# Node work between an attention and the edge sums of a graph network: two looped stages made into one written-out pipeline over 26 tiles

## The reference, cut to what matters

```python
# end of L0: agg = sum over a node's edges of alpha * message, (n, 256)
out = _typed_matmul(agg, a_linears, node_type)        # one of 4 weights, by the node's type
out = sigmoid(skip)[node_type][:, None] * out
x = x + out                                           # called x1 in the kernel

# L1, on h = relu(layernorm(x1)); row, col = src, dst
xt = (h @ weight).reshape(-1, 4, 64)
alpha_l = einsum('ehd,hd->eh', xt[row], attn_l)
alpha_r = einsum('ehd,hd->eh', xt[col], attn_r)
alpha = softmax(leaky_relu(alpha_l + alpha_r, 0.01), axis=1)     # over the 4 heads
tmp = einsum('nh,nhd->nd', alpha[:n], xt[col[:n]])    # only the first n = 3125 edges count
x = x + tmp broadcast over the 4 heads                # x2

# start of L2, on h = relu(layernorm(x2)), called h2
hs = h * rsqrt(clip(deg_out, 1))[:, None]             # rows that the edge sums gather (table2)
m = segment_sum(hs[src], dst) ...                     # sum_items, not changed
```

## Time and profile before

| | us |
|---|---|
| median of 3 timed runs | 6702.11 (6691.39 to 6745.78) |
| the profiled execution, its own time | 6654.7 |
| its span | 6653.1 |
| TensorE (PE) busy in the span | 4281.8 (64%) |
| VectorE (DVE) busy | 3563.9 (54%) |
| ScalarE (ACT) busy | 2224.7 (33%) |
| GpSimd (POOL) busy | 3118.9 (47%) |

### The profile page before, as it was taken

The page is one execution under the profiler, slowest core; times in us unless marked ns, Lnnn a source line. Parts: engine busy times, 40 slices in busy tenths (PEclk is TensorE's granted clock), DMA queues, the critical chain, the costliest instruction groups (busy, mean ns, idle before and its releaser), DMA issues. The chain is left out here.

```text
span 6653.1 us, 94389 instructions
## 1 busy us (share of the span) xinstructions
PE 4281.8 (64%) x25484; PEld 3173.8 (48%) x25484; DVE 3563.9 (54%) x7285; ACT 2224.7 (33%) x7694; POOL 3118.9 (47%) x3164
## 2 busy tenths in 40 slices
PE   3898577777767305655555558884657677776754
PEld 2665455656545204443443447772225555555542
DVE  3454688888863442222221311114249999998875
ACT  1332466666652210000000112221115555555540
POOL 0340677777750127777777020002036666666620
PEclk8999788888889656677776879995668888888875
DMA  5333788888871224333334067832147777777752
GB/s 184 119 131 116 224 260 260 253 255 260 254 173 57 59 76 123 103 103 104 104 104 97 9 213 261 262 113 84 63 149 221 222 228 223 229 226 220 224 130 73
DMA packets 559988, 1092.90 MB, mean 164 GB/s; under 512 B 129764, under 2 KB 372456, under 8 KB 556061
## 3 DMA queue, kind: packets, MB, share of 16 engines
q0 software_dynamic: 204144, 617.42, 32.2%
q1 hardware_dynamic: 355434, 470.78, 21.7%
HBM read 973.54 MB, written 201.47 MB: 177 GB/s over the span
## 5 line engine op out<-in xcount | busy, mean ns | idle before, releaser
L738 POOL DMA_INDIRECT l3e_kv<-t_table,k_recs x912 | 986.9, 1082 | 489.0 <-issue 250.7
L1394 PE MATMUL l2e_pA<-l2e_row,l2e_oh 128*128 128x257 f32 x1824 | 691.1, 545 | 742.7 <-issue 474.3
L738 POOL DMA_INDIRECT l0e_kv<-t_table,k_recs x912 | 966.9, 1060 | 292.3 <-issue 258.1
L1348 POOL DMA_INDIRECT l2e_row<-t_table,l2e_idx x912 | 882.3, 967 | 278.5 <-issue 277.5
L1394 PEld LDWEIGHTS l2e_pA<-l2e_row,l2e_oh 128*128 128x128 f32 x1824 | 472.2, 271 | 961.3 <-issue 870.4
L1015 ACT ACTIVATE l0e_vw<-l0e_kv,l0e_w 128x64 f32<-128x64 f32 x2736 | 679.8, 334 | 0.1
L1015 ACT ACTIVATE l3e_vw<-l3e_kv,l3e_w 128x64 f32<-128x64 f32 x2736 | 679.8, 334 | 0.0
L924 PE MATMUL l3e_pQE<-l3e_qb,l3e_ohT 128*128 128x256 bf16 x2736 | 412.1, 311 | 389.7 <-issue 359.4
L1373 DVE SCALAR_TENSOR_TENSOR l2e_acc<-l2e_acc,k_itf,l2e_pA 128x257 f32<-128x257 f32 x228 | 109.9, 482 | 929.4 <-issue 872.6
L972 PE MATMUL l0e_pA<-l0e_vw,l0e_ohf 128*128 128x260 f32 x1824 | 545.4, 451 | 11.0 <-ACT l0e_vw L1015 7.8
L924 PEld LDWEIGHTS l3e_pQE<-l3e_qb,l3e_ohT 128*128 128x128 bf16 x2736 | 290.9, 109 | 485.7 <-issue 410.7
(11 more groups left out here) (456 smaller groups left out, 7447.4 us busy)
## 6 DMA issues: line engine op xcount, KB each, us to landing
exp_w<-in_L_gnn_w SPq DMA_DIRECT2D x224, 512.0 KB
t_table<-l0n_tab SPq DMA_DIRECT2D x26, 2048.0 KB, 6.9
l0e_qb<-t_q SPq DMA_DIRECT2D x228, 192.0 KB, 6.0
l3e_qb<-t_q SPq DMA_DIRECT2D x228, 192.0 KB, 4.1
t_agg<-l0e_acc SPq DMA_DIRECT2D x228, 130.0 KB
t_agg<-l3e_acc SPq DMA_DIRECT2D x228, 130.0 KB
l0e_drow<-t_drow SPq DMA_DIRECT2D x57, 512.0 KB, 6.5
l3e_drow<-t_drow SPq DMA_DIRECT2D x57, 512.0 KB, 6.3
```

The source lines that it names most:

```text
L738: pool.indirect_dma_start(kv[:, n % SK, g, :], None, table[:, :], bass.IndirectOffsetOnAxis(ap=K["recs"][:, n, g, ridx:ridx + 1], axis=0)) ...
L1348: pool.indirect_dma_start(row[:, s, g, 0:D], None, table[:, :], bass.IndirectOffsetOnAxis(ap=idx[:, i, g:g + 1], axis=0)).then_inc(row_rea ...
L1394: last = pe.matmul(pA[s % 2][:, 0:W], oh[:, s, g, :], row[:, s, g, :], start=(g == 0), stop=(g == G - 1))
```

## The change

`layer1_nodes` and `layer2_nodes` are replaced by one stage, `layer12_nodes`, written out over the 26 tiles instead of looping over 13 pairs.

- x1 stays on chip in `M["xx"]`, the tile that `route` uses later; the normalised rows go into `M["agg"]`, and h2 is left in `M["h2"]`. The masks and `rdego` are kept in `K` from `layer0_nodes` on, so the store of `dego`, the stores and loads of x1 and h2 and the later loads of the masks go (in `sum_items`, `combine` and per tile). `tmask` is still stored, for `layer0_nodes` itself.
- `ag` and x are loaded in 5 chunks (`AT`) of up to 6 tiles. `wx`, `att` and the edge ends are issued by ScalarE; the edge ends as two transfers of 3328 single numbers.
- The typed projection: VectorE only divides by the denominator, a chunk at a time (`scale`); 2 transposes a tile instead of 8; `pO` holds the products with all 4 weights (2 banks), and VectorE adds the four, each times its mask column, to x (`typed`: 4 scalar_tensor_tensor). The relu is done by ScalarE in the copy of the transposed h.
- The engines' programs are shifted against each other: in slot t TensorE transposes tile t, projects tile t - 1, transposes h of t - 3, projects it for t - 4.
- GpSimd waits for all table stores, then issues 52 gathers with no wait between them. VectorE works on groups of 4 tiles (`GT`): `scores`, `heads_mean`, `normal2`; ScalarE applies relu twice per tile (`positive`).

```diff
-            with nc.allow_non_contiguous_dma(reason="3328 degrees, once"):
-                sp.dma_start(T["rdego"].rearrange("(b p) c -> p (b c)", p=P), dego[:, :]).then_inc(stored, 16)
...
-            sp.wait_ge(stored, 32)
+            sp.wait_ge(stored, 16)
...
+def layer12_nodes(nc, A, T, K, M):
...
+        AT = (0, 2, 8, 14, 20, NBP)
+        GT = (0, 4, 8, 12, 16, 20, 24, NBP)
...
+        @block.sync
+        def _(sp):
+            for j, (a, b) in enumerate(zip(AT, AT[1:])):
+                sp.dma_start(big[:, a:b, 0:H * HV], chunk("agg0", a, b)).then_inc(ag_in[j], 16)
+                if j == 0:
+                    for c in range(2):
+                        sp.dma_start(wa[:, c, :, :], A["L0_gnn_a_linears"][:, c * P:(c + 1) * P, :].rearrange("t p n -> p t n")).then_inc(wa_in, 16)
+                sp.dma_start(x[:, a:b, :], chunk("x0", a, b)).then_inc(x_in[j], 16)
+            for t in range(NBP):
+                sp.wait_ge(tb_ready, t + 1)
+                sp.dma_start(rows(T["table1"], t * P), tb[:, t % TB, :]).then_inc(tb_out[t % TB], 16)
+                sp.dma_start(rows(T["tablel"], t * P), tb[:, t % TB, D:D + H]).then_inc(tb_out[t % TB], 16)
+            for j, (a, b) in enumerate(zip(GT, GT[1:])):
+                sp.wait_ge(x2_ready, j + 1)
+                sp.dma_start(chunk("x2", a, b), x[:, a:b, :]).then_inc(stored, 16)
+                sp.wait_ge(hs_ready, j + 1)
+                sp.dma_start(chunk("table2", a, b), hs[:, j % 2, 0:b - a, :]).then_inc(hs_out[j % 2], 16)
...
+        def _(pool):
+            pool.wait_ge(edges_in, 32)
+            for u in range(TB):
+                pool.wait_ge(tb_out[u], 32 * ((NBP - 1 - u) // TB + 1))
+            for t in range(NBP):
+                j = t // GW
+                pool.indirect_dma_start(gd[:, t, :], None, T["table1"][:, :], bass.IndirectOffsetOnAxis(ap=di[:, t:t + 1], axis=0)).then_inc(g_in[j], 16)
+                pool.indirect_dma_start(gs[:, t, :], None, T["tablel"][:, :], bass.IndirectOffsetOnAxis(ap=si[:, t:t + 1], axis=0)).then_inc(g_in[j], 16)
...
+            def typed(t):
+                j = next(j for j in range(NA) if t < AT[j + 1])
+                dve.wait_ge(x_in[j], 16)
+                dve.wait_ge(o_ps, t + 1)
+                for k in range(NT):
+                    last = dve.scalar_tensor_tensor(out=x[:, t, :], in0=pO[t % 2][:, k, :], scalar=K["mask"][:, t, 1, k:k + 1], in1=x[:, t, :],
+                                                    op0=ALU.mult, op1=ALU.add)
...
+            scale(0)
+            head_weights()
+            for t in range(NBP + 2):
+                for j in range(1, NA):
+                    if t == max(AT[j] - 4, 1):
+                        scale(j)
+                if 0 <= t - 1 < NBP:
+                    typed(t - 1)
+                if 0 <= t - 2 < NBP:
+                    normal(t - 2)
...
+            for j in range(NG + 1):
+                if j < NG:
+                    scores(j)
+                if j:
+                    normal2(j - 1)
+                if j < NG:
+                    heads_mean(j)
...
+            def outputs(t):
+                pe.wait_ge(aT_ready, t + 1)
+                if t >= 2:
+                    pe.wait_ge(x1_ready, t - 1)
+                for o in range(2):
+                    for c in range(2):
+                        last = pe.matmul(pO[t % 2][:, 2 * o:2 * o + 2, :].rearrange("p k n -> p (k n)"), aT[:, t % 2, c, :],
+                                         wa[:, c, 2 * o:2 * o + 2, :].rearrange("p k n -> p (k n)"), start=(c == 0), stop=(c == 1))
+                last.then_inc(o_ps, 1)
...
+            for t in range(NBP + 4):
+                if t < NBP:
+                    turned(t)
+                if t == 1:
+                    pe.wait_ge(wa_in, 32)
+                if 0 <= t - 1 < NBP:
+                    outputs(t - 1)
+                if 0 <= t - 3 < NBP:
+                    turned_h(t - 3)
+                if t == 4:
+                    pe.wait_ge(wx_ready, 1)
+                if 0 <= t - 4 < NBP:
+                    projected(t - 4)
...
+            act.dma_start(wx[:, :, 0:D], A["L1_gnn_weight"].rearrange("(c p) n -> p c n", p=P)).then_inc(wx_in, 16)
...
+            with nc.allow_non_contiguous_dma(reason="the ends of the first 3328 edges, once"):
+                for t, a in ((si, "src"), (di, "dst")):
+                    act.dma_start(t[:, :], A[a][0:NP].rearrange("(b p) -> p b", p=P)).then_inc(edges_in, 16)
+
+            def turned(t):
...
-            sp.dma_start(M["h2"][:, :, :], T["h2"].rearrange("(b p) n -> p b n", p=P)).then_inc(next_in, 16)
-            sp.dma_start(M["mk"][:, :, :], T["tmask"].rearrange("(b p) c -> p b c", p=P)).then_inc(next_in, 16)
...
-            sp.dma_start(mk[:, :, :], T["tmask"].rearrange("(b p) c -> p b c", p=P)).then_inc(c_in, 16)
```

More of the change, by code:

```diff
@@ L1072, in layer1_nodes @@
         pH = S.ps("pH", [P, 4, P])
         pX = [S.ps(f"pX{u}", [P, 512]) for u in range(2)]
[L1074 to L1078, removed]
+        wa_in, wx_in, edges_in, wx_ready, scaled = (S.sem(k) for k in ("wa_in", "wx_in", "edges_in", "wx_ready", "scaled"))
@@ L1079, in layer1_nodes, with chunk @@
+        hs_out = S.sems_of("hs_out", 2)
         block = S.block()
+        def chunk(name, a, b):
+            return T[name].rearrange("(b p) c -> p b c", p=P)[:, a:b, :]
         @block.sync
         def _(sp):
[L1083 to L1111, removed]
@@ L1130, in step @@
[L1130 to L1149, removed]
@@ L1151, in _, with scale @@
-            repeat(dve, NBP // 2, step)
+            def scale(j):
+                a, b = AT[j], AT[j + 1]
+                dve.wait_ge(ag_in[j], 16)
+                dve.tensor_scalar(rden[:, a:b, :], ag[:, a:b, :, DK], 1e-30, None, ALU.max)
+                dve.drain()
+                dve.reciprocal(rden[:, a:b, :], rden[:, a:b, :])
+                dve.drain()
+                dve.tensor_tensor(h[:, a:b, :].rearrange("p b (h d) -> p b h d", h=H), ag[:, a:b, :, 0:DK],
+                                  rden[:, a:b, :].unsqueeze(3).to_broadcast([P, b - a, H, DK]), ALU.mult).then_inc(scaled, 1)
@@ new lines, in head_weights @@
+            def head_weights():
+                dve.wait_ge(wx_in, 48)
+                for c in range(2):
+                    for j in range(2):
+                        dve.tensor_tensor(wtmp[:, c, j, :], wx[:, c, 0:D], att[:, j, :], ALU.mult)
+                dve.drain()
+                for c in range(2):
+                    for j in range(2):
+                        last = dve.tensor_reduce(wx[:, c, D + j * H:D + (j + 1) * H], wtmp[:, c, j, :].rearrange("p (h d) -> p h d", h=H), AX.X, ALU.add)
+                last.then_inc(wx_ready, 1)
@@ new lines, in normal2 @@
+            def normal2(j):
+                a, b = GT[j], GT[j + 1]
+                dve.wait_ge(root2_ready, j + 1)
+                dve.reciprocal(mv2[:, a:b, 3], mv2[:, a:b, 2])
+                dve.drain()
+                for t in range(a, b):
+                    dve.tensor_scalar(h[:, t, :], x[:, t, :], mv2[:, t, 0:1], mv2[:, t, 3:4], ALU.subtract, ALU.mult).then_inc(n_ready, 1)
+            for j in range(NG + 1):
[5 more added lines that the diff above has]
+                    heads_mean(j)
@@ new lines, in turned_h, with projected @@
+            def turned_h(t):
+                pe.wait_ge(h_ready, t + 1)
+                if t:
+                    pe.wait_ge(hT_ready, t)
+                for c in range(2):
+                    last = pe.transpose(pH[:, c, :], h[:, t, c * P:(c + 1) * P], K["ident"][:, :])
+                last.then_inc(h_ps, 1)
+            def projected(t):
+                pe.wait_ge(hT_ready, t + 1)
+                if t >= 2:
+                    pe.wait_ge(tb_ready, t - 1)
+                for c in range(2):
+                    last = pe.matmul(pX[t % 2][:, 0:WX], hT[:, t % 2, c, :], wx[:, c, :], start=(c == 0), stop=(c == 1))
+                last.then_inc(x_ps, 1)
@@ new lines, in projected @@
+            def projected(t):
+                act.wait_ge(x_ps, t + 1)
+                if t >= TB:
+                    act.wait_ge(tb_out[t % TB], 32 * (t // TB))
+                act.activation(tb[:, t % TB, :], pX[t % 2][:, 0:WX], ACT.Copy).then_inc(tb_ready, 1)
+            for t in range(NBP + 4):
+                if t < NBP:
+                    turned(t)
+                if 0 <= t - 2 < NBP:
+                    rooted(t - 2)
+                if 0 <= t - 3 < NBP:
+                    turned_h(t - 3)
+                if 0 <= t - 4 < NBP:
+                    projected(t - 4)
```

317 lines of the change are left out of this document (135 added, 182 removed).

## The result

| | before | after |
|---|---|---|
| median of the runs first shown, us | 6699.26 (4 runs) | 6394.82 (4 runs, 6391.19 to 6416.98) |
| the profiled execution | 6654.7 | 6391.2 (span 6389.5) |

The ratio is 0.9555, 95% interval 0.9514 to 0.9595.

A forecast was written before the change was run, and what follows sets the result against it. No engine was full; chains of waits set the 506 us of node work. Gains of 252 us there and 17.5 elsewhere took 6654.7 to 6385, shifted by 47 to 6432 us; range 6365 to 6490.

The forecast's parts named there:

- stretch: From the first transfer of `layer12_nodes` to the start of `sum_items`: 254 us against 506, 252 us gained.
- Head: First transfer of the new stage to its first `pO`, ScalarE's queue held by single-number loads: 21 us.
- Steady part: The slots of the 26 tiles after the first `pO`, TensorE bounding each at 4.95 us: 135 us.
- Turn: From the last `pO` on, GpSimd waiting for every table store before gathering: 10 us with nothing beside it.
- Phase 2: 52 gathers back to back beside VectorE's groups of four tiles, VectorE just the later: 88 us.
- Degree store: End of `layer0_nodes` without the `dego` store, which took 19.5 us to land: 13.5 us gained (12 to 15).
- combine: In `combine`, where the mask load stood ahead of the x2 load: 3 us gained (0 to 6).
- The shift of 47 us: Whole kernel: timed runs' median 47 us above the profiled execution, so the sum went from 6385 to 6432 us.
- A: Head and feed slow, loads number by number crowding the chunk stream: 6455 to 6460 us; chance 0.10.
- B: TensorE loses its clock in the new slots: 6452 us at 0.90, 6561 at 1.2 GHz; chance 0.10.
- C: Pipeline doesn't overlap, in-order engines waiting for each other in every slot, 9.6 us each: 6553 us; chance 0.04.
- D: Gathers starve beside a packed VectorE, 2.83 + 0.30 us each: 6527 us; chance 0.03.

The follow-up runs named there:

- Experiment 1: Changed kernel without the shift between engines, every engine doing all steps of a tile before the next: 6674.7 us, stretch 457.1 us.
- 2: Changed kernel with half the typed projection on TensorE left out: `pO` every 3.38 to 3.52 us, typed projections 96.7 us.
- 3: Changed kernel with GpSimd waiting, before each group's eight gathers, for x2 of the group before: phase 2 131.5 us (88.9).
- 6: Changed kernel with the edge-end loads issued by GpSimd instead of ScalarE: first `pO` after 12.8 us (13.9), stretch 251.1 us.
- 12: Changed kernel with `tm` and `al` in PSUM, `normal2` ahead of `scores`, edge ends issued by GpSimd: 6393.42 us, ratio to before 0.9545.
- 4: Changed kernel with `tm` and `al` in PSUM: gathers 64.7 us in all, phase 2 84.7 us.
- 5: Changed kernel with `tm` alone in PSUM: gathers 68.1 us in all, phase 2 86.7 us.
- experiment 8: Changed kernel with the store of `dego` put back: last table store to first gather 25.4 us, against 11.0 in the changed kernel.
- Experiment 9: Changed kernel with h2 and the masks through DRAM again: phase 2 105.5 us (103.1 in the set), `sum_items` 1321.4, `combine` 115.7.

## Why the prediction was right, and which terms were off

- **The mechanism** held: stretch 237.9 to 239.0 where I had 254 (and said 245 to 265 for "right"). Experiment 1 shows the overlap, 2 that TensorE sets the slot, 3 the back-to-back gathers.
- **The sum came out near partly by luck.** On the profile's scale I had 269.5 us gained and the profiles give 263.6, but the terms miss both ways: the stretch gave 16.4 more, the end of `layer0_nodes` 9.5 less, the first attention lost 6.4 that I had at nothing, and all behind the stretch lost 2.4 where I had 4 gained.
- **One reading of before was wrong.** I put 480.6 us of GpSimd's waiting into `layer2_nodes`, which lasted 251. Its last gather of the attention ended at 1936.6, so of the 306.5 us ahead of its first gather only some 4 lie in that stage; inside it GpSimd waited some 178 us. No term of the sum used the 480.6.
- **Head** 13.9 for 21. The step "ScalarE's queue is held" is in the trace (10.65 us for my 13.6), but I added 5 us of sharing on top, which no run shows. The queue set the end; the landing of the weights stood right behind it, due one to two microseconds earlier (experiments 6 and 12). The value near the lower bound was the right choice, with the 15.6 us of before as the nearest row.
- **Steady part** 121.9 for 135. The slot is 4.77, not 4.95: near the 4.7 I gave for the case that all tails overlap. The first and the last slots, with nothing of h to transpose or project, are shorter (3.65 and 4.08 us for the second and third), which I did not count: some 4 us. One `scale` lump shows (a slot of 5.45), not four.
- **Turn** 13.1 for 10. Left without work between dependent steps, TensorE ran the last projections at a granted clock of 0.78 over the turn; the last store, issued at 2131.57, let the first gather go at 2135.20.
- **Phase 2** 88.9 for 88, but partly by luck. "VectorE just the later, over 90% busy" was wrong: 65% busy, a group 9.6 us rather than 10.7, and GpSimd sets the pace, with gathers at a mean of 1.04 for my 1.00. That 1.00 came from `combine`, where the long gathers are held in the same way (experiments 4 and 5). Here the long ones add 4.8 us, 0.09 to the mean of 52.
- **Degree store** 13.5: measured 14 (experiment 8). In the first profile only 4.0 were left, since the last table store went out 9.8 us later, at 663.27 for 653.45, in a `layer0_nodes` granted 0.76 from 150 to 200 us where the one before had 1.00.
- **sum_items** 1: lost 1.3. **combine** 3: gained 0.8. Experiment 9 prices all this traffic at 3.
- **The shift of 47 us** was the term that missed most: the changed kernel's median lies 3.6 us above its profile, not 47, which is 43 us of a miss of 37 in all. I took a gap between one profile and three runs as a property of the scale. For the larger part it was a state of `layer0_nodes` in that execution (33.8 of the 54.4 us between the two profiles of before); the rest is spread over the later stages. The first gain between medians was 304, the second 281; the profiles' own 263.6 and 289.4.
- **Rivals.** A fell (head 13.9). B did not come in phase 1 (0.99), though `layer0_nodes` has such executions; the rule of the Trainium skill in "TensorE: Matmul & The Clock Gate", section "A second HAM failure mode: psum-queue depth-cycling", has no case in the changed stage. C came true as soon as the shift was taken away, and at 13.6 us a slot rather than my 9.6. D fell (longest gather 1.71 in the changed kernel's stage).

## What to carry to other kernels

When a loop over tiles passes each tile through four engines, count the slot of each engine and shift their programs until the slowest never waits: here the smaller work of phase 1 without the shift took longer than the kernel before, and with it 106 us less. Beside gathers issued by GpSimd, give VectorE's wide two-input instructions one operand in PSUM (5 us here). And compare two profiles only after checking that the granted clock in the stages *not* changed is the same; a state there moved 34 us here from one execution to the next.

## What the runs showed of the hardware

- A gather that begins during a product or addition of VectorE with both inputs in SBUF ends 0.80 to 0.83 us after that instruction ends (70 of 70); with one operand in PSUM it takes 0.94 to 0.95. The normalisation, with one wide input, does the same to gathers that begin 0.14 us or more into it (19); reductions and statistics do not (0 of 109).
- TensorE at 62% busy was granted 0.75 over 346 us; the same work in 121.9 us, hardly ever idle, 0.99.
- `layer0_nodes` runs from 550 to 650 us at 1.00 in some executions and at 0.78 in others, with the same program.
- Of two loads of 3328 single numbers each, the issue of the second stands 10.65 us on ScalarE's queue, and the copy behind it waits; on GpSimd's the two issues took 1.55 and 1.53.
